# A graph layer over a dense adjacency: two short tail groups replaced by one loop over sixteen equal groups

## What is computed

```python
agg = adj @ (x @ W_agg)
y = x + w[:, None] * relu(agg) + (1.0 - w)[:, None] * x
out = (y - mean(y, axis=-1)) / sqrt(var(y, axis=-1) + 1e-5)
```

## Time and profile before

| | us |
|---|---|
| median of 3 runs | 638.62 |
| the 3 runs | 640.05, 638.62, 638.38 |
| the profiled execution's own time | 638.89 |
| its span | 637.0 |
| PE matmul busy | 519.5 (82%) |
| DVE busy | 55.8 (9%) |
| ACT busy | 15.9 (2%) |
| mean granted TensorE clock | 0.912 of full speed |
| DMA | 272.75 MB, mean 428 GB/s |

### The profile page before, as it was taken

One profiled execution on the slowest core, in us unless ns is written; L12 is line 12 of the kernel. 1 busy time (PEld: TensorE's weight loads), 2 busy tenths in 40 slices (PEclk: granted clock), 3 DMA queues, 4 the chain that ended last, 5 costly groups with the idle time before them and its releaser, 6 DMA issues.

```text
span 637.0 us, 5371 instructions
## 1 busy us (share of the span) xinstructions
PE 519.5 (82%) x2304; PEld 177.2 (28%) x2304; DVE 55.8 (9%) x136; ACT 15.9 (2%) x35; POOL 0.3 (0%) x5
## 2 busy tenths in 40 slices
PE   0678798878987888797878977878887987978996
PEld 0123232222222322222222322322222222222345
DVE  2000101010010100101001010100101001010102
ACT  0000000000000000000000000000000000000000
POOL 0000000000000000000000000000000000000000
PEclk9997898888979889897988979898888989888999
DMA  9999999999999999999999999999999999999998
GB/s 362 453 418 453 419 427 433 425 447 428 444 414 447 419 429 443 441 432 419 451 410 436 436 450 423 427 431 425 446 424 453 424 429 419 436 444 420 428 413 349
DMA packets 9667, 272.75 MB, mean 428 GB/s; under 512 B 1472, under 2 KB 1728, under 8 KB 3008
## 3 DMA queue, kind: packets, MB, share of 16 engines
q1 hardware_dynamic: 9360, 272.63, 99.6%
q10 hardware_dynamic: 304, 0.07, 0.1%
HBM read 270.60 MB, written 2.10 MB: 428 GB/s over the span
## 4 chain that ended last, share of the span: by engine, by line
DMA 69%; PE 29%; issue 0%; SPq 0%; ACT 0%; DVE 0%; DVEq 0%
DMA ring<-adj_main_dram 69%; PE bank L156 29%; PE bank L164 0%; SPq L114 0%; ACT aggT L203 0%; ACT aggT L208 0%; SPq L110 0%; SPq L109 0%; DVE res L267 0%; ACT std_last L199 0%; DVE y_last L261 0%; ACT aggT L211 0%; DVE stats L263 0%; DVE y_last L262 0%; DVE mv L264 0%
## 5 line engine op out<-in xcount | busy, mean ns | idle before, releaser
L156 PE MATMUL bank<-ring,x_sb 128*64 128x512 f32 (+2 forms) x2176 | 501.7, 621 | 102.2 <-DMA ring<-adj_main_dram 102.1
L156 PEld LDWEIGHTS bank<-ring,x_sb 128*64 128x64 f32 x2176 | 161.6, 148 | 430.2 <-issue 299.7
L245 DVE SCALAR_TENSOR_TENSOR y<-bank,w_sb 128x256 f32<-128x256 f32 (+1 forms) x16 | 6.7, 420 | 552.7 <-PE bank L164 552.7
L164 PE MATMUL bank<-wagg,aggT 128*128 128x64 f32 x128 | 17.9, 281 | 11.2 <-ACT aggT L203 10.3
L164 PEld LDWEIGHTS bank<-wagg,aggT 128*128 128x128 f32 x128 | 15.6, 191 | 25.4 <-ACT aggT L203 23.5
L203 ACT COPY aggT<-bank 128x512 f32<-128x512 f32 x15 | 8.8, 585 | 527.0 <-PE bank L156 527.0
L234 DVE TENSOR_TENSOR y<-y,res 128x256 f32<-128x256 f32 (+1 forms) x16 | 6.7, 420 | 2.2
L242 DVE TENSOR_TENSOR res<-y,rstd 128x256 f32 (+1 forms) x16 | 6.7, 421 | 0.6
L238 DVE TENSOR_TENSOR sq<-y 128x256 f32<-128x256 f32 (+1 forms) x16 | 6.7, 421 | 0.6
L236 DVE SCALAR_TENSOR_TENSOR y<-rowsum,y 128x256 f32<-128x256 f32 (+1 forms) x16 | 6.7, 420 | 0.5
L239 DVE TENSOR_REDUCE varsum<-sq 128x4 f32<-128x256 f32 (+1 forms) x16 | 6.7, 416 | 0.5
(11 more groups left out here) (9 smaller groups left out, 1.3 us busy)
## 6 DMA issues: line engine op xcount, KB each, us to landing
ring<-adj_main_dram SPq DMA_DIRECT2D x30, 5632.0 KB, 27.2
ring<-adj_main_dram SPq DMA_DIRECT2D x15, 5120.0 KB, 29.8
ring<-adj_mid_dram SPq DMA_DIRECT2D x2, 2304.0 KB, 22.8
ring<-adj_mid_dram SPq DMA_DIRECT2D x1, 3072.0 KB, 21.5
ring<-adj_mid_dram SPq DMA_DIRECT2D x2, 1536.0 KB, 23.9
x_sb<-x_dram SPq DMA_DIRECT2D x1, 2048.0 KB, 8.0
out_dram<-res SPq DMA_DIRECT2D x1, 2016.0 KB, 8.1
ring<-adj_last_dram SPq DMA_DIRECT2D x2, 768.0 KB, 23.0
```

The costliest lines, as they stand in the source:

```text
L156: last = nc.tensor.matmul(into[j % 2 * D:(j % 2 + 1) * D, 0:cols], x_sb[:, j], ring[:, at + s * cols:at + (s + 1) * cols], start=j < 2, st ...
L164: last = nc.tensor.matmul(rows[:, i * D:(i + 1) * D], aggT[:, i * P:(i + 1) * P], wagg2[:], start=True, stop=True)
L245: step(nc.vector.scalar_tensor_tensor(out=y[:, 0:n], in0=rows.rearrange("p (n d) -> p n d", d=D), scalar=0.0, in1=over_row(w_sb[:, bass.ds ...
```

## The change

All 64 row tiles are worked as sixteen groups of four (14 in `adj_main`, one in `adj_mid`, one in `adj_last`; the host arrays keep their three names), and PE, ACT and DVE each run one loop of sixteen. The code for three tiles and for one tile goes, with its PSUM banks and small tiles. `adj_mid` is loaded like a main group, in three DMAs of 22, 22 and 20. `adj_last` is loaded in ten pieces: 12 and 10, 12 and 10, and 7, 5, 3, 2, 2, 1 source tiles. The first piece of a chunk signals `loaded[c]`; each other piece has a semaphore. As PE's loop is the same for all groups, PE waits for these semaphores in every group: POOL raises each once at the start (seven one-column memsets), which meets the wait for groups 0 to 14 (value 1), and in group 15 the wait is for 17. ACT copies the accumulator in four instructions of 128 columns, each with its own signal, and PE's turn-back matmul i waits for copy i. PE's waits for x and W_agg move into the loop.
The diff, cut to its core:

```diff
-MID_SLOTS = 3
-LAST_SLOTS = 1
+MID_SLOTS = 4
+LAST_SLOTS = 4
 SUB = 64
-MAIN_LOADS = (22, 22, 20)
-MID_LOADS = (16, 12, 12, 8, 8, 4, 2, 2)
-LAST_LOADS = (10, 12, 12, 10, 7, 5, 4, 2, 2)
+LAST_PIECES = ((12, 10), (12, 10), (7, 5, 3, 2, 2, 1))
...
-    MID, LAST = G, G + 1
+    MAIN = adj_main.shape[0]
+    G = MAIN + 2
+    LAST_T0 = T - LAST_SLOTS
...
+    LOADS = [sum(pieces) for pieces in LAST_PIECES]
+    C = len(LOADS)
+    SLOT = max(LOADS) * COLS
...
+        ones = sb("ones", [P, sum(len(pieces) - 1 for pieces in LAST_PIECES)])
...
+        rows_ps = bank[:, 1, 0:MAIN_SLOTS * D]
...
-        mid_loaded = [sem(f"mid_loaded{k}") for k in range(len(MID_LOADS))]
-        last_loaded = [sem(f"last_loaded{k}") for k in range(len(LAST_LOADS))]
+        piece_loaded = [[sem(f"piece_loaded{c}{k}") for k in range(1, len(pieces))] for c, pieces in enumerate(LAST_PIECES)]
...
+            def load(c, group):
+                j, n = sum(LOADS[:c]), LOADS[c]
+                sp.dma_start(ring[:, c * SLOT:c * SLOT + n * COLS], group[:, :, j:j + n].rearrange("o q s n -> (o q) (s n)")
                              ).then_inc(loaded[c], 16)
...
+            with sp.Fori(1, MAIN) as g:
                 for c in range(C):
                     sp.wait_ge(slot_free, g * C + (c + 1 - C))
+                    load(c, adj_main[bass.ds(g, 1), 0])
+            for c in range(C):
+                sp.wait_ge(slot_free, MAIN * C + (c + 1 - C))
+                load(c, adj_mid[0:1])
             j = 0
-            for k, n in enumerate(LAST_LOADS):
-                sp.dma_start(ring[:, LAST_AT + j * P:LAST_AT + (j + n) * P],
-                             adj_last[:, j:j + n].rearrange("q s n -> q (s n)")).then_inc(last_loaded[k], 16)
-                j += n
-            sp.wait_ge(out_ready, LAST)
+            for c, pieces in enumerate(LAST_PIECES):
+                sp.wait_ge(slot_free, (MAIN + 1) * C + (c + 1 - C))
+                at = c * SLOT
+                for k, n in enumerate(pieces):
+                    sp.dma_start(ring[:, at:at + n * COLS], adj_last[:, j:j + n].rearrange("q s n -> q (s n)")
+                                 ).then_inc(piece_loaded[c][k - 1] if k else loaded[c], 16)
+                    j, at = j + n, at + n * COLS
+            sp.wait_ge(out_ready, G - 1)
             sp.dma_start(out_rows[:, 0:LAST_T0], res[:, 0:LAST_T0]).then_inc(stored, 16)
...
+            for k, piece in enumerate(sum(piece_loaded, [])):
+                nc.gpsimd.memset(ones[:, k:k + 1], 1.0).then_inc(piece, 1)
...
+            with nc.Fori(0, G, engines=[mybir.EngineType.PE], head_slot={mybir.EngineType.PE: 200}) as g:
+                pe.wait_ge(x_in, 16)
+                pe.wait_ge(wagg_in, 32)
+                j = 0
+                for c, pieces in enumerate(LAST_PIECES):
+                    pe.wait_ge(loaded[c], g * 16 + 16)
+                    at = c * SLOT
+                    for k, n in enumerate(pieces):
+                        if k:
+                            pe.wait_ge(piece_loaded[c][k - 1], (g + 1) // G * 16 + 1)
+                        last = contract(at, j, n)
+                        j, at = j + n, at + n * COLS
+                    last.then_inc(slot_free, 1)
+                pe.wait_ge(dve_step, g * DVE_GROUP + DVE_PRE)
+                for i in range(MAIN_SLOTS):
+                    pe.wait_ge(agg_copied, g * MAIN_SLOTS + (i + 1))
+                    last = nc.tensor.matmul(rows_ps[:, i * D:(i + 1) * D], aggT[:, i * P:(i + 1) * P], wagg2[:], start=True, stop=True)
                 last.then_inc(rows_done, 1)
-            with pe.Fori(0, G) as g:
...
-                turn_back(rows_ps, MAIN_SLOTS, g + 1)
...
-                nc.scalar.copy(aggT[:], acc).then_inc(agg_copied, 1)
-                std_of(std[:], varsum[:], 1.0 / D, g * DVE_GROUP + (DVE_PRE + VAR_STEP))
+                for i in range(MAIN_SLOTS):
+                    nc.scalar.copy(aggT[:, i * P:(i + 1) * P], acc[:, i * P:(i + 1) * P]).then_inc(agg_copied, 1)
+                act.wait_ge(dve_step, g * DVE_GROUP + (DVE_PRE + VAR_STEP))
+                nc.scalar.activation(std[:], varsum[:], ACT.Sqrt, bias=eps[:, 0:1], scale=1.0 / D).then_inc(std_ready, 1)
                 act.wait_ge(out_ready, g + 1)
-            act.wait_ge(mid_done, 1)
-            nc.scalar.copy(aggT[:, 0:MID_COLS], mid_acc).then_inc(agg_copied, 1)
-            std_of(std[:, 0:MID_SLOTS], varsum[:, 0:MID_SLOTS], 1.0 / D, MID * DVE_GROUP + (DVE_PRE + VAR_STEP))
-            act.wait_ge(last_done, 1)
-            nc.scalar.copy(aggT[:, 0:P], last_acc).then_inc(agg_copied, 1)
-            std_of(std_last[:], mv[:, 1:2], 1.0, LAST_STEP0 + LAST_VAR_STEP)
-            act.wait_ge(out_ready, LAST + 1)
...
+                residual = res[:, bass.ds(g * MAIN_SLOTS, MAIN_SLOTS)]
                 dve.wait_ge(rows_done, g + 1)
-                weigh(rows_ps, g * MAIN_SLOTS, MAIN_SLOTS, base)
-                normalise(g, g * MAIN_SLOTS, MAIN_SLOTS, base)
-            base = MID * DVE_GROUP + DVE_PRE
-            dve.wait_ge(rows_done, MID + 1)
-            weigh(mid_rows, MID_T0, MID_SLOTS, base)
-            normalise(MID, MID_T0, MID_SLOTS, base)
-            v, t = y_last[:], LAST_T0
-            dve.wait_ge(rows_done, LAST + 1)
-            step(nc.vector.tensor_scalar(v, last_rows, 0.0, w_sb[:, t:t + 1], ALU.max, ALU.mult), LAST_STEP0 + 1)
-            step(nc.vector.tensor_tensor(v, v, res[:, t], ALU.add), LAST_STEP0 + 2)
-            step(nc.vector.bn_stats(stats[:], v), LAST_STEP0 + 3)
-            step(nc.vector.bn_aggr(mv[:], stats[:]), LAST_STEP0 + LAST_VAR_STEP)
-            dve.wait_ge(std_ready, LAST + 1)
-            step(nc.vector.reciprocal(rstd_last[:], std_last[:]), LAST_STEP0 + 5)
-            nc.vector.tensor_scalar(res[:, t], v, mv[:, 0:1], rstd_last[:, 0:1], ALU.subtract, ALU.mult).then_inc(out_ready, 1)
+                step(nc.vector.scalar_tensor_tensor(out=y[:], in0=rows_ps.rearrange("p (n d) -> p n d", d=D), scalar=0.0,
+                                                    in1=over_row(w_sb[:, bass.ds(g * MAIN_SLOTS, MAIN_SLOTS)]),
+                                                    op0=ALU.max, op1=ALU.mult), base + 1)
+                step(nc.vector.tensor_tensor(y[:], y[:], residual, ALU.add), base + 2)
+                step(nc.vector.tensor_reduce(rowsum[:], y[:], AX.X, ALU.add), base + 3)
+                step(nc.vector.scalar_tensor_tensor(out=y[:], in0=over_row(rowsum[:]), scalar=-1.0 / D, in1=y[:],
+                                                    op0=ALU.mult, op1=ALU.add), base + 4)
+                step(nc.vector.tensor_tensor(sq[:], y[:], y[:], ALU.mult), base + 5)
+                step(nc.vector.tensor_reduce(varsum[:], sq[:], AX.X, ALU.add), base + VAR_STEP)
+                dve.wait_ge(std_ready, g + 1)
+                step(nc.vector.reciprocal(rstd[:], std[:]), base + DVE_GROUP)
+                nc.vector.tensor_tensor(residual, y[:], over_row(rstd[:]), ALU.mult).then_inc(out_ready, 1)
```

More of the change, by code:

```diff
@@ L96, in gnn_residual_layernorm @@
         eps_ready = sem("eps_ready")
-        mid_done, last_done = sem("mid_done"), sem("last_done")
         agg_copied = sem("agg_copied")
@@ L115, in main_load @@
                              ).then_inc(loaded[c], 16)
             for c in range(C):
-                main_load(c, adj_main[0:1, 0])
-            with sp.Fori(1, G) as g:
+                load(c, adj_main[0:1, 0])
+            with sp.Fori(1, MAIN) as g:
                 for c in range(C):
                     sp.wait_ge(slot_free, g * C + (c + 1 - C))
[L123 to L131, removed]
-                j += n
@@ L145, in _, with contract @@
             nc.gpsimd.memset(eps[:], EPS).then_inc(eps_ready, 1)
+            for k, piece in enumerate(sum(piece_loaded, [])):
+                nc.gpsimd.memset(ones[:, k:k + 1], 1.0).then_inc(piece, 1)
         @block.tensor
         def _(pe):
-            pe.wait_ge(x_in, 16)
-            pe.wait_ge(wagg_in, 32)
-            def contract(into, at, cols, j0, n):
+            def contract(at, j0, n):
                 for s in range(n):
                     j = j0 + s
-                    last = nc.tensor.matmul(into[j % 2 * D:(j % 2 + 1) * D, 0:cols], x_sb[:, j],
-                                            ring[:, at + s * cols:at + (s + 1) * cols], start=j < 2, stop=j >= T - 2)
-                return last
@@ L160, in turn_back @@
[L160 to L164, removed]
-                last.then_inc(rows_done, 1)
-            with pe.Fori(0, G) as g:
[L168 to L172, removed]
-                turn_back(rows_ps, MAIN_SLOTS, g + 1)
@@ L174, in _ @@
-            j = 0
-            for k, n in enumerate(MID_LOADS):
-                pe.wait_ge(mid_loaded[k], 16)
-                last = contract(mid_acc, j * MID_COLS, MID_COLS, j, n)
-                j += n
-            last.then_inc(mid_done, 1)
-            turn_back(mid_rows, MID_SLOTS, MID + 1)
-            j = 0
```

(18 more changed lines are left out.)

43 lines of the change are left out of this document (3 added, 40 removed).

## The result

| | median us | runs | span of the profiled execution |
|---|---|---|---|
| before | 638.88 | 638.38 to 640.05 (5) | 637.0 |
| after | 642.08 | 641.94 to 642.12 (5) | 640.3 |

The changed kernel takes 1.0043 of the time of before (95% interval 1.0032 to 1.0054): 3.2 us more by the medians, 3.3 us by the spans. The forecast was 642.0 us and a span of 640.3 to 640.4.

What follows compares the result with a forecast made beforehand. Loads were taken to bound the kernel, with a serial tail behind the last landing. Stream -0.4, PE +0.75, copies +0.84, DVE +1.9, store and loop end +0.3: 3.4 us on 638.62, forecast 642.0 us, range 640.0 to 643.9.

Steps and rivals of the forecast that it cites:

- Part 1: Load stream up to the last landing: steady groups unchanged, seven more DMAs at 0.061 us, landing at 631.17, 0.4 us won.
- Part 2: PE behind the last piece: it keeps up with the loads and ends 1.2 us behind the last landing, at 632.4.
- one of the named signs: Profile readings named in advance; this one had PE's clock at full speed from 583 us to the end.
- Rival A: PE's clock falls in the last chunk, if idles near 612 and 618 exceed 2 us: +1.7, 643.7 us; chance 10%.
- the replay: PE's last group worked through ahead: start at 602.5, idles of some 0.8 and 0.9 us, last chunk met on time.
- The lone tile priced as a pair: Last piece on PE: one source tile alone takes 0.86 us in its half of PSUM, not 0.43.
- Part 3: Copy and turn-back in the tail: four copies take 1.15 us, then 0.52 to DVE's first step, at 634.1.
- its sign of 1.15 us: Profile reading for the last group's tail: the four ACT copies should take 1.15 us.
- Part 4: DVE's steps on four tiles in the tail: 3.89 us against 2.00 for one tile, 1.9 more; ends at 638.0.
- Part 5: Last store: 2.05 us as now, plus 0.2 for the larger store and 0.1 for the loop's end.
- part 6: Loop placement, extra waits, memsets, register work and dropped code cost nothing, lying beside the first load or PE's stalls.
- Rival B: Not slower: the last load lands earlier, below 630, as the slowest DMA engine's lag goes; 640.0 to 639.2 us; chance 17%.

Runs made afterwards that it cites:

- e6: The changed kernel with the last group loaded in whole chunks of 22, 22 and 20 source tiles; 649.17 us.
- e12: The changed kernel with the last chunk in pieces of 5, 5, 4, 2, 2, 2 in place of 7, 5, 3, 2, 2, 1; 641.74 us.
- e4: The changed kernel with one ACT copy of 512 columns and one wait of PE in place of four copies; 642.33 us.
- e1: The changed kernel without a chosen place for PE's loop in the program; 642.07 us.
- e2: The changed kernel with PE's loop begun at instruction 239 of a block in place of 200, so that it reaches into a third block; 642.18 us.
- e5: The changed kernel with DVE's and ACT's steps of every group on the first of its four tiles alone; 640.60 us.
- e9: The kernel before, unchanged, profiled once more; its profiled execution took 640.04 us, in the upper cluster, span 638.2.
- e11: The kernel before with SP's store cut from 63 tiles to one; 638.79 us, ratio 1.0004.

## Why the prediction was right

Step by step, forecast against measured:

| step | forecast | measured |
|---|---|---|
| last landing | 631.17 | 631.1 |
| from there to PE's last matmul | 1.2 | 1.3 |
| from that matmul to DVE's first step | 1.72 | 1.60 |
| DVE and the square root | 3.89 | 3.90 |
| to the store's issue | 0.13 | 0.16 |
| issue to the end of the span | 2.25 | 2.26 |
| span | 640.3 to 640.4 | 640.3 |

Part 1 held: the steady groups were left as they are (553.07 to 591.85 is 38.78 us), and the landing moved by the number of DMAs: 631.1 - 591.85 = 39.25 us for the last group, forecast 39.22, and 0.07 us a DMA by e6. The store of 60 tiles is through 2.4 us before the last one is issued.

Part 2 held in its result and had one error in its course, and with it one of the named signs was missed, that the clock would stand at full speed from 583 on. PE did not start the last group at 602.5 but at 603.86, because of the fall of the clock in the chunk before. Rival A named such a fall as dangerous only in the last group; it came one chunk earlier and was taken up by the idles that the replay had counted. The reason given against A, that the idle of 0.77 ahead of 591.95 had no fall after it, was read from one profile; in this one the idle there was 2.46, and the fall came. A's own condition, an idle beyond 2 us, is no safe sign either: there was none after 2.33 and one after 1.37. The lone tile priced as a pair is borne out by e12.

Part 3 was too dear by 0.12, and came so close by two errors that offset each other. Copies on end do not take 0.30 each: the four records of 0.28 stand in 0.77 us, not 1.15, so they start 0.16 apart. But from the last copy's end (633.18) to DVE's first step stand 0.80 us, not 0.52, since what binds is not the last copy but the turn-back, 1.10 us for its eight matmuls behind the first copy. The path was wrong there, and its sign of 1.15 us missed. e4 gives what the split is worth.

Part 4 held to 0.01 us, as it had rows of the same operations on the same shape. Part 5 held to 0.03, though its two additions, 0.1 for the loop's end and 0.2 for the larger store, had no such row: measured were 0.13 and 0.21. Of part 6, e1 and e2 tested the place of the loop; the waits, the memsets and the code that went were not tested one by one, but the period of 38.78 us leaves no cost for them in the steady groups, and the steps of the table none in the tail.

Rival B is out: the stream did not come in earlier than the count of its pieces says.

The sum in the prediction has 0.84 for the copies where its own terms give 4 x 0.265 + 3 x 0.03 - 0.265 = 0.89; in the total of 3.4 this is lost in the rounding.

What the prediction left out is that the time of before has two values, since its PE works without slack at the end. The spans compared, 637.0 and 640.3, take the lower one. Against it the change costs 3.3 us; against the upper one, 638.2, it costs 2.1 us. The median of 638.88 with 642.08 gives 3.2, and it would shift with the share of upper runs. The mechanism accounts for the 3.3 us; that the forecast of 642.0 came within 0.1 is also luck. Its base was the median of three runs, one of them in the upper cluster (640.05); with two there it would have been over 639.3 and the forecast 642.7 or more. And the steps, each off by up to 0.12 us, erred to both sides.

## What to carry to other kernels

When a stream of loads sets the pace to its end, the price of a change at the end is the serial work behind the last landing, and it can be added up from rows of the same operations, here to about 0.1 us a step; here a last group of four tiles costs 3.3 us more than one of one tile, with the 0.5 us that fewer loads give back already taken off. A time with two clusters is worth a look at slack: an engine that never waits in the last stretch passes most of a fall of its clock on to the end (here 1.4 of 1.7 us), and pieces that let it start earlier give it room.

## What the runs showed of the hardware

- A fall of TensorE's clock in a chunk of 20 source tiles costs 1.7 us (10.50 against 8.80). In 6 of the 14 profiles (e1, e5, e9, e11, e12 and the changed kernel) it came between 591.8 and 593.1, in the chunk before the last 39 us of loads, each time after an idle of 2.46 to 2.48 us and a chunk at full clock. The two of them with PE's code of before (e9, e11) have spans of 638.2, against 636.8 to 637.0 of its other three; among those of the changed kernel's code and pieces there is no such step (640.3 with the fall in the changed kernel and e1, 640.4 without it in e2).
- Four ACT copies of 128 columns from PSUM start 0.16 us apart though each record lasts 0.28 (four in 0.77 us); one copy of 512 columns takes 0.59.
- PE's loop of some 283 instructions over three blocks of its program ran 15 jumps back with two instruction packets in the whole span (e2), against one with the loop at 200.
- Cutting the stream into more DMAs costs it 0.07 us for each: the last landing is at 630.6 with 3 DMAs in the last group (e6) and at 631.1 with 10.
